# A bias row added by accumulating transfers instead of by VectorE, in a fused graph network kernel

## The reference

```python
def layer(h, W, q, k, b):                      # relational attention, 8 relations
    xw = einsum('nf,rfg->rng', h, W)
    out_j, out_i = xw[edge_type, src], xw[edge_type, dst]
    alpha = segment_softmax(leaky_relu(out_i @ q + out_j @ k), dst)
    return segment_sum(alpha * out_j, dst) + b

x = layernorm(x + mean_of_messages(x, edge_attr, src, dst))
h = relu(layer(x, W[0], q[0], k[0], b[0]))
h = relu(layer(h, W[1], q[1], k[1], b[1]))
return layernorm(x + h)
```

## Time and profile before

| what | value |
|---|---|
| median of the runs | 973.25 us (969.68 to 974.24) |
| span of the profiled execution | 970.2 us (the record gives no other time of it) |
| VectorE busy | 807.0 us, 83% |
| TensorE busy | 681.9 us, 70% |
| ScalarE busy | 613.2 us, 63% |
| GpSimd busy | 586.1 us, 60% |
| line 1065, the bias row | 40 times, 59.4 us |
| gathers of the two layers, line 461 | 98 and 98, 130.4 and 136.3 us |

### The profile page before, as it was taken

The page is one execution under the profiler, slowest core; times in us unless marked ns, Lnnn a source line. Parts: engine busy times, 40 slices in busy tenths (PEclk is TensorE's granted clock), DMA queues, the critical chain, the costliest instruction groups (busy, mean ns, idle before and its releaser), DMA issues.

```text
span 970.2 us, 11352 instructions
## 1 busy us (share of the span) xinstructions
PE 681.9 (70%) x3092; PEld 444.5 (46%) x3092; DVE 807.0 (83%) x2191; ACT 613.2 (63%) x1396; POOL 586.1 (60%) x506
## 2 busy tenths in 40 slices
PE   3646656646664499999897888559999998678300
PEld 2425545534543355555464556536555554334200
DVE  4589998888899799988999998488979889999940
ACT  1569997979998766656666676456566553433540
POOL 4767777777770588887700000088888765666774
PEclk9658776877776599999999999569999999989755
DMA  8266757656653323232644376223231251132110
GB/s 224 84 203 200 203 178 226 186 156 202 199 159 124 124 96 101 67 124 73 225 127 139 98 211 176 69 91 101 66 127 44 71 180 42 44 122 88 48 44 28
DMA packets 87770, 123.01 MB, mean 127 GB/s; under 512 B 14188, under 2 KB 66854, under 8 KB 87707
## 3 DMA queue, kind: packets, MB, share of 16 engines
q1 hardware_dynamic: 69483, 99.36, 32.3%
q0 software_dynamic: 15680, 21.55, 7.9%
q10 hardware_dynamic: 2544, 1.38, 0.6%
HBM read 87.79 MB, written 45.05 MB: 137 GB/s over the span
## 4 chain that ended last, share of the span: by engine, by line
DVE 28%; POOL 24%; issue 17%; PE 15%; ACT 7%; DMA 6%; SPq 1%; POOLq 0%; DVEq 0%; ACTq 0%
POOL xs L461 17%; PE ps_y L714 6%; POOL xd L461 6%; DVE work L1295 5%; DVE ys L1121 5%; ACT stage L795 3%; DVE st L1102 2%; DVE ys L1268 2%; DVE opT L1295 2%; DVE st L1071 2%; POOL out L530 2%; DMA xs<-h_table,posI 2%; PE ps_t L680 1%; DVE st L1061 1%; DVE xd L1274 1%
## 5 line engine op out<-in xcount | busy, mean ns | idle before, releaser
L795 ACT ACTIVATE stage<-stage,nm,rs 128x128 f32<-128x128 f32 x800 | 319.6, 483 | 23.2 <-DVE nm L1056 21.6
L714 PE MATMUL ps_y<-work,wr 128*128 128x512 f32 (+1 forms) x528 | 228.0, 562 | 32.7 <-DVE work L1295 32.7
L461 POOL DMA_INDIRECT xs<-h_table,posI x98 | 136.3, 1391 | 176.1 <-DMA h_table<-ys 146.5
L461 POOL DMA_INDIRECT xs<-x_table,posI x98 | 130.4, 1331 | 63.1 <-DMA x_table<-xd 33.5
L714 PEld LDWEIGHTS ps_y<-work,wr 128*128 128x128 f32 x528 | 97.1, 195 | 127.7 <-issue 68.5
L1295 DVE SCALAR_TENSOR_TENSOR work<-typB,xs 128x896 f32<-128x896 uint8 x132 | 142.6, 1086 | 13.3 <-ACT xs L760 7.3
L530 POOL DMA_INDIRECT out<-xd,outI x98 | 108.4, 1106 | 56.5 <-issue 28.3
L461 POOL DMA_INDIRECT xs<-in_x,srcI x98 | 104.7, 1069 | 47.3 <-issue 28.3
L714 PE MATMUL ps_y<-opT,wr 128*128 128x512 f32 (+1 forms) x256 | 115.0, 574 | 16.8 <-DVE opT L1295 16.7
L461 POOL DMA_INDIRECT xd<-in_x,dstG x98 | 104.3, 1064 | 30.1 <-issue 29.6
L1061 DVE BATCH_NORM_STATS2 st<-stage 128x6 f32<-128x128 f32 x400 | 82.9, 278 | 21.0 <-DMA stage<-in_x 20.5
(11 more groups left out here) (206 smaller groups left out, 1115.5 us busy)
## 6 DMA issues: line engine op xcount, KB each, us to landing
stage<-in_x SPq DMA_DIRECT2D x39, 640.0 KB, 4.0
out<-stage SPq DMA_DIRECT2D x39, 640.0 KB, 3.1
xs<-alpha_rows SPq DMA_DIRECT2D x28, 448.0 KB, 5.3
x_table<-xd SPq DMA_DIRECT2D x14, 448.0 KB, 3.1
h_table<-ys SPq DMA_DIRECT2D x14, 448.0 KB, 3.5
work<-in_src SPq DMA_DIRECT2D x13, 448.0 KB, 5.3
ys<-in_edge_attr SPq DMA_DIRECT2D x6, 896.0 KB, 8.6
sameB<-same_rows SPq DMA_DIRECT2D x42, 112.0 KB
```

The source lines that it names most:

```text
L461: nc.gpsimd.indirect_dma_start(out=buf[:, t, :], out_offset=None, in_=table, in_offset=bass.IndirectOffsetOnAxis(ap=idx[:, t:t + 1], axis= ...
L714: mm = pe.matmul(ps_y[:, u, lo:hi], wr[:, r, :], rows, start=(r == 0), stop=(r == R - 1))
L795: ins = a.activation(slot(c)[:, r, :], slot(c)[:, r, :], ACT.Identity, bias=nm[:, h, n:n + 1], scale=rs[:, h, n:n + 1])
```

## The change

The bias row, clipped at zero and repeated ten times, is first stored to a table in device memory. In the two layers GpSimd then issues, for each bulk step there, a transfer that reads this table for every partition and adds it to the slot in place. VectorE's addition at r = 3 is gone for these steps, and ahead of its second statistics at r = 4 it waits for the transfer. GpSimd issues the transfer for step K_M[j] + m behind the gather of group min(7m // 5 + 3, 13): behind groups 3, 4, 5, 7, 8, 10, 11, 12, and then five behind group 13 in layer 0, and behind groups 3, 4, 5, 7, 8, 10 and 11 in layer 1. Before each it waits for the table and for the first normalisation. The other 20 bulk steps still add on VectorE.

```diff
@@ -97,6 +97,7 @@
     h1_table = nc.dram_tensor("h1_table", (EP, D), F32).ap()
     typ_rows = nc.dram_tensor("typ_rows", (TL, P), U8).ap()
     same_rows = nc.dram_tensor("same_rows", (TL, P), U8).ap()
+    relu_rows = nc.dram_tensor("relu_rows", (BR, D), F32).ap()
     alpha_rows = nc.dram_tensor("alpha_rows", (TL, P), F32).ap()
 
     with ExitStack() as ctx:
@@ -237,6 +238,7 @@
         pro = sem("dve_steps")
 
         b_sum = sem("b_sum"); b_sd = sem("b_sd"); b_rs = sem("b_rs"); b_norm1 = sem("b_norm1"); b_norm2 = sem("b_norm2")
+        rows_r = sem("rows_r"); shift_in = sem("shift_in")
 
         p_step = sem("p_step"); p_row = sem("p_row"); p_ready = sem("p_ready")
 
@@ -271,6 +273,7 @@
         src_pad = src.unsqueeze(0)
         typ_flat = typ_rows.rearrange("t p -> (t p)").unsqueeze(0)
         same_flat = same_rows.rearrange("t p -> (t p)").unsqueeze(0)
+        relu_flat = relu_rows.rearrange("r d -> (r d)").unsqueeze(0)
         alpha_flat = alpha_rows.rearrange("t p -> (t p)").unsqueeze(0)
 
         Q16 = QF // 16 * 16
@@ -358,6 +361,8 @@
             for k in range(1, K_A):
                 bulk_step(k)
             edges(1)
+            sp.wait_ge(bsum_r, 1)
+            sp.dma_start(relu_rows, relu_row[0:BR, 1, :]).then_inc(rows_r, 16)
             typ_spread(0)
             typ_spread(1)
             for g in range(NG + 1):
@@ -496,6 +501,12 @@
                 elif n == 2 * G - 1:
                     pool.wait_ge(f_q[0], i)
 
+            def shift_rows(k):
+                pool.wait_ge(rows_r, 16)
+                pool.wait_ge(b_norm1, k)
+                b = (k - 1) % SLOTS
+                nc.gpsimd.dma_start(stage[:, b * BR * D:(b + 1) * BR * D], relu_flat.to_broadcast([P, BR * D]), accum_op=ALU.add).then_inc(shift_in, 16)
+
             pool.wait_ge(src_r, 1)
             for g in range(NG):
                 if g == 1:
@@ -520,6 +531,9 @@
                 for g in range(NG):
                     pool.wait_ge((a_norm, refill)[j], g + 1 if j == 0 else REFILLS.index(g) + 1)
                     gather(g, xs, (x1_table, h1_table)[j], posI, xs_in[j + 1], EP - 1)
+                    for m in range(K_E[j] - K_M[j]):
+                        if min(7 * m // 5 + 3, NG - 1) == g:
+                            shift_rows(K_M[j] + m)
             for b in range(SLOTS):
                 pool.wait_ge(bulk_out[b], 16 * len(range(b, BC + 1, SLOTS)))
             for g in range(NG):
@@ -1089,9 +1103,8 @@
             def bulk_piece(n, k):
                 if 0 < n < 3:
                     bulk_first(k, range((n - 1) * BR // 2, n * BR // 2))
-                elif n == 3:
-                    bulk_shift(k)
                 elif n == 4:
+                    dve.wait_ge(shift_in, 16 * (1 + sum(m < k for j in range(2) for m in range(K_M[j], K_E[j]))))
                     bulk_second(k)
                     bulk_sums(k)
                 elif n == 6:
```

## The result

The kernel with the change takes 1068.27 us (median of 4; 1063.49 to 1071.51), the kernel before 973.75 us in the same series. The ratio is 1.0973, with a 95% interval of 1.0923 to 1.1023: about 95 us slower. The forecast was 1080 us.

The account below looks back on a forecast made before the run. VectorE, with 27.7 us idle over the changed stretch, was taken as the bound. 25.3 + 36.4 + 25.2 + 26.0 - 12 + 6 = 107 us on 970.2 gave 1077, with 3 for the median 1080 us; range 1005 to 1170.

Parts of the forecast that it names:

- the first stalls: VectorE's wait for the first transfer of each layer, issued late by GpSimd: 25.3 us in layer 0, 25.2 in layer 1.
- P: Price of one transfer, from first normalisation done or GpSimd free to VectorE going on: 9.4 us, ends 3.6 and 17.4.
- The first term: First transfer of each layer, issued only behind gather group 3, reaches VectorE late: 25.3 us in layer 0, 25.2 in layer 1.
- The second term: The other 18 transfers, whose latency exceeds the slack before the second statistics: 36.4 us in layer 0, 26.0 in layer 1.
- the rule of that term: Each later step costs the larger of -1.4 us and P less its slack between first normalisation and second statistics.
- after the first stall GpSimd is ahead: Later steps: GpSimd no longer late, so statistics, root, scales, normalisation and transfer form the chain; 36.4 and 26.0 us.
- The third term: Across both layers: stalls swallow 12 of VectorE's 27.7 us idle, TensorE's clock returns cost 6 us, gather effects count nothing.
- A: Rival: short transfer, P about 5.4 us; first stalls remain, other steps nearly cancel; +34 us, 1007 us; chance 0.18.
- B: Rival: long transfer, P about 17.4 us, from slow adding or one shared address range; +267 us, 1240 us; chance 0.15.
- C: Rival: not slower, first stall paid from VectorE's idle time, P at 3.6 us, no clock loss; 966 us; chance 0.05.

## Why the prediction was right, step by step

The time and the order of the causes were right, and the first stalls came about as forecast. Inside the sum the price was too high and a loss was missing, and they made up for each other. With 6.1 us for P the same sum gives 22.0 + 21.9 + 7 - 12 + 6 = 45 us, which is 1018 us. It is still inside the range, but that 1080 came within 12 us of the measured 1068 is luck.

**The first term** was 25.3 and 25.2 us; it came out as 21.8 and 22.5. The mechanism is as forecast: the issue left only behind group 3, 37.8 us after the first gather of layer 0, where 38.1 was worked out (39.1 for 38.1 in layer 1). What is too large is P, 9.4 us against 6.1 (362.40 to 368.47). Of the 3.3 us, about 2.2 are the landing, taken as 8 and measured as 5.8, and the rest is the issue, which I counted once more although "issue to landing" in the earlier trace rows holds it. The landing was too large because I let the broadcast of the earlier trace rows count: with rows of its own a transfer is not faster but slower by 0.4 us. And reading the old values costs 1.5 us, not 2.3.

**The second term** was 36.4 + 26.0 us, of which 12 - 6 were to come back, 56.4 in all; it came out as 26.6 + 22.9 = 49.5. This looks right and is not. By the rule of that term and the P measured, each step would lose the larger of -1.4 and 6.1 less its slack, and that adds up to 7 us over 18 steps. The step that failed is "after the first stall GpSimd is ahead": at m = 3 and 5 in both layers it is not, since two groups of gathers stand ahead of the transfer. Placing the issues evenly took off 10.1 us in layer 0 (253.4 to 243.3) and 13.4 in layer 1 (124.7 to 111.3), 23.5 of the 49.5. The issues two groups earlier, which left those two places as they are, took off only 3.0.

The rest, some 19 us beyond the rule, is open, but the timelines of ScalarE and GpSimd say where in the loop it lies. The prediction took the time from the second statistics to the end of the next first normalisation as unchanged. With the full change it is 11.5 us longer over the 18 steps together, but with evenly placed issues only 0.8 us, and there the 19 us are still lost ("later" is 26.0 us longer than before the change, where the rule gives 7). So they lie behind the normalisation. There 0.5 us pass before the issue (381.97 to 382.50; 0.1 was taken), and where VectorE waits for a transfer it goes on 5.6 to 8.3 us after the issue, with evenly placed issues 5.7 to 9.2, not always 6.1. Why some take longer no run shows. For the later steps I have also seen the waits of masks for TensorE (30.5 us in all, 6.2 before) and the lower clock (0.90 and 0.87), but no run takes them away by themselves. The length of the first stall is not the reason: at m = 1 of layer 0 the time to the first normalisation was 11.2 us (344.76 to 355.93); it is 13.5 behind a wait of 22.6 us (368.47 to 381.97), and 13.1 and 13.4 in the two kernels whose first wait is 6.8 us.

**The third term.** The clock dipped as said; what that cost is not measured by itself. Waits for loads fell, by 9.4 us; swallowed idle time was taken as 12. GpSimd lost its gather issues of 3 to 4 us: 14 of the 196 in the two layers took more than 2.5 us before, and none takes more than 1.92 after. The gathers were busy for 107.3 and 109.9 us against 130.4 and 136.3, 49.5 us less, which is more than the 19.4 us of the new issues. I see no gain from it in the table, where both layers are longer.

**The rivals.** A (short transfer, 1007 us) had P nearly right, 5.4, and the time wrong by 60 us, for the reason of the second term. B (a slow addition) is refuted by 5.8 us. C (made up later) is refuted: "from there to the end" is the same to 0.5 us. Expectations of the profile: waits of about 25 us (22.6 and 23.4), later ones of 2 to 6 (0.4 to 8.3, and none at m = 9 to 11 in layer 0 and m = 6 in layer 1), landing of 6 to 13 (5.8, just below), a busy time of VectorE down by 29.7 (25.9).

**The two rules weighed.** "DMA: Bandwidth & Descriptors" in the Trainium skill (Anatomy of one DMA) gave 3.5 us for the transfer as an estimate; without the addition it measured 4.3, with it 5.8. "SBUF — State Buffer" in the Trainium skill (Who interferes with whom) has GpSimd's reads of SBUF held off by VectorE instructions with two SBUF inputs. The gather that started at 341.70 in the changed kernel agrees: with no addition beside it, it took 1.66 us instead of 4.07.

## What to carry to other kernels

Before work is moved to an engine with free time, ask where in that engine's order the new instruction would stand at the moment when its result is wanted. Here GpSimd's share was 60%, and yet it was 20 us behind at the start of each layer, and two groups of gathers stood ahead of the transfer at two later places of each. An operation of 1.5 us inside a loop over three engines is not replaced by one of 6 us unless the loop has that much slack, read between the producer's end and the consumer's start step by step and not from shares. And a stall can cost a little more than its length: what stands behind it drains, and here the next step took some 2 us longer to come round, behind a wait of 6.8 us as behind one of 22.6.

## What the runs showed of the hardware

- An accumulating transfer of 640 KB into SBUF lands in 5.8 us (5.5 to 8.2), the same without the addition in 4.3 us (3.8 to 7.9); a shared source of 5 KB is no slower than 640 KB of distinct rows (5.8 against 6.2).
- GpSimd needs 0.99 us to issue the accumulating transfer, whether it moves 64 KB or 640 KB, and 0.58 us to issue the plain one of 640 KB.
- An increment that stands behind GpSimd's 28th gather of layer 0 reached VectorE eleven gather issues ahead of that gather.
- A gather's issue of 1.00 us on GpSimd took 4.07 us while VectorE ran an addition between two masks, 1.66 us where the addition was gone.
